# Ranks stage of a Perceiver-Mamba kernel: where key rows lie, which engine folds weights, and how the counting loops are written

## The chip, the cores and the metric

One core of a Trainium2 chip runs the whole program in one launch. The metric is the device time of one execution in microseconds. Five engines run at once, each through its own list of instructions, and are tied together by semaphores: TensorE (PE, with its weight loads PEld), VectorE (DVE), ScalarE (ACT), GpSimd (POOL) and SyncE (SP), which here only issues transfers. ScalarE issues a few transfers too.

## The reference

A layer of three blocks works on 16 x 32 tokens of 512 channels: a point-cloud cross attention, a Mamba-2 block and a small gated feed-forward. Only the start of the first block matters here. Its coordinates are three rows of the context; they are quantised to 10 bits, turned into four space-filling-curve keys per point (two Morton, two Hilbert), and each key list is sorted:

```
def _sorted_indices(coords_bn3):
    q = _quantize(coords_bn3)
    qt = q[..., jnp.array([1, 0, 2])]
    keys = [_morton_key(q), _morton_key(qt), _hilbert_key(q), _hilbert_key(qt)]
    return [jnp.argsort(kk, axis=1) for kk in keys]
...
x = x + _L0_xattn_ref(ctx_4096, _layernorm(x, axis=-1), ...)
```

The sorted order is used to gather windows of 10 neighbours out of the layer-normed `x` (the latents). `W_lin1`, `W_lin2` with `W_conv1`, `W_conv2` follow; since they are linear one after the other they can be multiplied together beforehand.

## The kernel before

The function `keys_and_ranks` is the first stage; barriers and cleared semaphores separate it from the next, `gather_windows`. It never sorts. It finds the rank of every key by comparing it with all the others of its list: 16 batches of 512 keys for each of 4 curves.

**Keys.** VectorE quantises, spreads bits and forms the Morton keys (`pieces(0)`), then the Hilbert keys (bit loops, then `pieces(1)`). A key is cut into three fp16 pieces plus an index row, four rows in all (`p16`). SyncE stores them in DRAM (`store_keys`, L200) and they come back transposed by `load_keys` (L188): into `mv_key` and `st_key`, four small transfers of two partitions for each curve, so eight for the Morton pair (four issued by SyncE, four by ScalarE) and eight for the Hilbert pair (all on SyncE). Curve m has its eight rows at partitions 32m to 32m+7: key rows in one tile face constant rows in the other, which ScalarE filled before (L318).

**Differences.** TensorE multiplies eight rows of `st_key` by eight of `mv_key` (L268): the product at (i, j) is key j minus key i. By symmetry only the upper triangle is made, 512, 384, 256 and 128 columns for tiles 0 to 3, of both curves of a pair. These lie in three PSUM banks (`TURNS`: tile 0, tile 1, tiles 2 and 3).

**Counting.** For the first nine Morton batches (`SOLO`) ScalarE takes the sign of both curves with a row sum (L332). After that a batch is shared: ScalarE takes curve one (L340 Morton, L348 Hilbert), VectorE compares curve two with zero and counts (L496, L504). I call the 7 Morton and 16 Hilbert batches of this kind the shared batches, 23 in all. TensorE then adds up columns of the signs for the other triangle (`column_sums`, L282, one column each). The two engines' counting loops are hardware loops (`Fori`) whose waits and addresses are computed from a loop register. TensorE's part is written out. TensorE waits until a bank is counted before it writes it again, and takes column sums two steps behind the differences.

**Work on the side.** Layer norm of the latents: VectorE makes statistics, ScalarE the root, VectorE then writes `latn` (L470) after the Hilbert keys. Folded weights: TensorE multiplies them at the start (L238 to L242), and after `latn` VectorE scales them by their largest entry and splits them (L478 to L487), 18 instructions for two layers. TensorE transposes the result two steps into the Hilbert half (L303), and VectorE copies that out after its last count (L509, L542, L543). VectorE's order is a list written by hand: Hilbert keys, `latn`, weights, shared Morton batches, Hilbert batches, weight copies, and last the ranks from counts and column sums (L516 to L528). GpSimd has nothing to do in the stage.

## Time and profile before

| what | us |
|---|---|
| median of three runs (lowest, highest) | 2252.63 (2251.91, 2253.1) |
| the profiled execution | 2251.6 |
| its span | 2249.8 |
| VectorE begins to write `latn` | 64.37 |
| first count by VectorE | 71.07 |
| last count by VectorE ends | 118.8 |
| first VectorE instruction of the next stage | 126.14 |

The span is what the profiler saw between the first and the last instruction, and the execution's time is 1.8 us more. All times below are from the span's start. In the timeline a piece's start and length are given, and in brackets how long the engine was idle before it and who released it. A matmul's end is modelled, so that starts are the better measure on TensorE. The stage at issue is the first 126 us; in it TensorE's granted clock is at its full level throughout. The chain that the page gives as having ended last covers only the last stage, and so this stage has to be read from timelines and waits.

### The profile page before, as it was taken

Reading aid. Unit: us, or ns where it says so; the run is one execution under the profiler, and the core shown is the slowest. Engines: PE = TensorE matmul, PEld = TensorE weight load, DVE = VectorE, ACT = ScalarE, POOL = GpSimd, SP = SyncE. Lnnn points to the kernel's source line nnn. Section 1 sums busy time; section 2 is a strip of 40 time slices with the busy share of each in tenths; the row PEclk is TensorE's granted clock in tenths of the full one; section 3 lists DMA queues with packets and bytes.
Section 4 is the critical chain, followed back from the end, with each engine's and each line's share of the span. In section 5 each row is a group of like instructions: output and inputs, shape, how many; then the busy total and the mean of one; then the engine's idle time right before and its main releaser. Section 6 shows DMA issues by size and latency. Waiting matters only on the chain. (4 is left out here: it accounts for less than half of the span.)

```text
span 2249.8 us, 100270 instructions
## 1 busy us (share of the span) xinstructions
PE 1857.1 (83%) x37656; PEld 1296.1 (58%) x37656; DVE 1865.7 (83%) x3775; ACT 1620.7 (72%) x3324; POOL 1007.2 (45%) x995
## 2 busy tenths in 40 slices
PE   3866648888886665699999997687999999999957
PEld 1333347777775433599999996333544454454422
DVE  8879969999997798688888887865888888888874
ACT  5889948888886998699999996465455455555432
POOL 0000048999995000578888884002433444344412
PEclk9996679999998666899999998899999999999988
DMA  1127666555563477645555551203222222222210
GB/s 36 30 65 169 163 146 126 119 125 122 120 125 72 94 171 164 133 101 107 107 107 107 107 107 38 95 10 96 85 80 84 75 84 81 82 84 75 65 55 19
DMA packets 434892, 215.50 MB, mean 96 GB/s; under 512 B 301195, under 2 KB 404267, under 8 KB 434680
## 3 DMA queue, kind: packets, MB, share of 16 engines
q1 hardware_dynamic: 430272, 210.76, 39.8%
q10 hardware_dynamic: 4536, 3.66, 0.6%
q8 instruction: 48, 0.79, 0.2%
q14 instruction: 36, 0.29, 0.0%
HBM read 161.35 MB, written 52.86 MB: 95 GB/s over the span
## 5 line engine op out<-in xcount | busy, mean ns | idle before, releaser
L973 PE MATMUL pQ<-QM,QX 128*128 128x64 f16 (+1 forms) x5760 | 532.4, 217 | 1.6 <-issue 1.6
L971 PE MATMUL pQ<-neigh_lo,QX 128*128 128x32 f16 (+1 forms) x5760 | 520.9, 189 | 2.8 <-issue 2.8
L971 PEld LDWEIGHTS pQ<-neigh_lo,QX 128*128 128x128 f16 x5760 | 496.0, 103 | 5.2 <-issue 2.5
L973 PEld LDWEIGHTS pQ<-QM,QX 128*128 128x128 f16 x5760 | 487.8, 104 | 2.5 <-issue 2.3
L1069 POOL TENSOR_TENSOR Dm<-Sc,mx 128x450 f32<-128x450 f32 x384 | 365.9, 953 | 80.6 <-DVE mx L1029 80.6
L1076 POOL TENSOR_TENSOR Ap<-E,R 128x450 f32<-128x450 f32 x384 | 365.8, 953 | 68.0 <-DVE R L1042 57.8
L1106 ACT ACTIVATE Vs<-pQ 128x480 f32<-128x480 f32 (+1 forms) x384 | 295.7, 770 | 5.7 <-PE pH L999 4.1
L1038 DVE STREAM_TRANSPOSE AT<-Ap 128x480 f32<-128x480 f32 x384 | 259.2, 675 | 33.3 <-PE pH L999 10.9
L2067 POOL TENSOR_TENSOR MT<-cb,decay 128x512 f32 (+1 forms) x128 | 163.9, 1302 | 244.2 <-PEq L1835 147.4
L1119 ACT ACTIVATE E<-Dm 128x450 f32<-128x450 f32 x384 | 224.3, 584 | 60.5 <-POOL Dm L1069 60.4
L1029 DVE TENSOR_REDUCE mx<-Sc 128x15 f32<-128x450 f32 x384 | 223.8, 583 | 16.5 <-ACT Sc L1100 16.5
L1033 DVE TENSOR_REDUCE Z<-E 128x15 f32<-128x450 f32 x384 | 233.5, 608 | 0.0
L1100 ACT ACTIVATE Sc<-pQ 128x450 f32<-128x450 f32 x384 | 209.2, 545 | 14.7 <-PE pQ L973 14.6
L999 PE MATMUL pH<-AT,Vs 128*32 128x30 f32 x17280 | 177.2, 197 | 47.5 <-DVE AT L1038 41.9
L999 PEld LDWEIGHTS pH<-AT,Vs 128*32 128x32 f32 x17280 | 172.5, 110 | 67.8 <-DVE AT L1038 42.0
L707 DVE TENSOR_TENSOR QT<-ext,cen 128x1710 f16<-128x1710 f32 x96 | 180.6, 1936 | 28.5 <-ACT ext L795 23.9
L966 PE MATMUL pQ<-maskR,maskL 128*128 128x160 f16 (+1 forms) x960 | 143.1, 247 | 67.5 <-DMA QX<-scratch_q 40.5
L2082 POOL TENSOR_TENSOR sqsum<-sqsum,sq 128x512 f32<-128x512 f32 x56 | 85.0, 1518 | 245.4 <-ACT sq L1928 245.4
L1860 PE MATMUL pO<-Wo,yw 128*128 128x512 f16 x768 | 176.3, 379 | 13.9 <-DVE Wo L2025 13.9
L1842 PE MATMUL pG<-h,W 128*128 128x512 f16 x768 | 178.2, 382 | 9.3 <-DVE W L2049 8.4
L2035 DVE SCALAR_TENSOR_TENSOR cv_m<-pX,taps_m,cv_m 128x496 f32<-128x496 f32 (+2 forms) x192 | 137.6, 717 | 51.7 <-ACT cv_m L1937 33.5
L1942 ACT ACTIVATE hid<-cv_m 128x512 f32<-128x512 f32 x64 | 40.3, 630 | 189.5 <-DVE cv_m L2035 189.5
(382 smaller groups left out, 3743.3 us busy)
## 6 DMA issues: line engine op xcount, KB each, us to landing
QM<-scratch_q SPq DMA_DIRECT2D x192, 240.0 KB, 2.7
QX<-scratch_q SPq DMA_DIRECT2D x768, 60.0 KB, 2.4
scratch_q<-QT SPq DMA_DIRECT2D x120, 360.0 KB, 4.8
Wg<-in_in_proj SPq DMA_DIRECT2D x64, 256.0 KB, 2.7
Wh<-in_in_proj SPq DMA_DIRECT2D x64, 256.0 KB, 2.8
Wo<-in_out_proj SPq DMA_DIRECT2D x64, 256.0 KB, 2.7
W_s<-in_in_proj SPq DMA_DIRECT2D x16, 256.0 KB, 2.7
CT<-scratch_c SPq DMA_DIRECT2D x192, 11.2 KB, 2.2
```

The costliest lines, as they stand in the source:

```text
L707: v.tensor_tensor(flat[:, 0:W3, n * K:(n + 1) * K, :], rows(ext, k, LEAD * K + HALF - 1 + n, (PTS * RES, W3), (1, K), (PTS, RES)), rows(ce ...
L971: nc.tensor.matmul(pQ[:, p, u // PB, o + 32:o + BW], qx[u], W["neigh_lo"][:, 0:O], start=False, stop=True, skip_group_check=True)
L973: last = nc.tensor.matmul(pQ[:, p, u // PB, o:o + BW], qx[u], qm[u], start=False, stop=True, skip_group_check=True)
L999: last = nc.tensor.matmul(pH[at0:at0 + 32, p, 32 * u:32 * u + PTS * K], Vs[:, first + slot, u * O + 32 * half:u * O + 32 * half + 32], AT[ ...
L1029: v.tensor_reduce(mx[:, p, :], valid(Sc[:, p, :]), X, ALU.max).then_inc(max_ready, 1)
L1033: v.tensor_reduce(Z[:, p, :], valid(E[:, p, :]), X, ALU.add).then_inc(summed, 1)
L1038: v.transpose(AT[:, k5 % NA, :], A[:, k5 % ND, :]).then_inc(turned, 1)
L1069: nc.gpsimd.tensor_tensor(valid(Dm[:, p, :]), valid(Sc[:, p, :]), mx[:, p, :].unsqueeze(2).to_broadcast([128, SUBS, PTS * K]), ALU.subtrac ...
L1076: nc.gpsimd.tensor_tensor(valid(A[:, p, :]), valid(E[:, p, :]), R[:, p, :].unsqueeze(2).to_broadcast([128, SUBS, PTS * K]), ALU.mult).then ...
L1100: nc.scalar.activation(like(Sc[:, (k - 1) % ND, :], 32, PTS * K), blocks(p, 0, PTS * K), ACT.Copy)\
L1106: nc.scalar.activation(like(Vs[:, kv % RV, :], O, O), blocks(p, 32, O), ACT.Copy).then_inc(vs_ready, 1)
L1119: nc.scalar.activation(valid(E[:, p, :]), valid(Dm[:, p, :]), ACT.Exp, scale=32.0 ** -0.5).then_inc(exped, 1)
```

## The change

Four things change, all in `keys_and_ranks` and its constants.

1. `load_keys` moves all eight rows of a curve pair in one transfer. They now lie eight partitions apart (`mv_key` at 0, 8, ..., 56, `st_key` at 4, 12, ..., 60, plus 64 for the Hilbert pair). A pair needs two transfers instead of eight. The constants `units` are laid out accordingly, with zeros elsewhere, and each difference now contracts 32 rows instead of 8.
2. The counting loops of ScalarE and VectorE are written out, with constants in their waits. `SOLO` goes from 9 to 10, so 22 batches are shared.
3. GpSimd writes `latn`, scales and splits the folded weights, copies the transposed ones out, and makes the Morton ranks. Since it works from SBUF, ScalarE copies the folded product (`raws`) and the transposed weights (`sides`) out of PSUM. VectorE takes the two maxima and reciprocals at once, ahead of the Morton keys.
4. TensorE transposes the weights before the first difference. Column sums of the Hilbert pair go to the bank `pw`; VectorE copies the Morton sums out (`early`) after its second Hilbert batch, and at the end finishes the Hilbert ranks alone.

```diff
-        SOLO = 9
+        SOLO = 10
...
-        def load_keys(eng, m):
-
-            for h in range(2):
-                for tile, at in ((mv_key, 32 * m + 4 * h), (st_key, 32 * m + 4 * h + 2)):
-                    eng.dma_start(tile[at:at + 2, :, 0:N],
-                                  scratch["pk"][m, 2 * h:2 * h + 2, :].rearrange("r (b n) -> r b n", b=B))\
-                        .then_inc(keys_in[m // 2], 16)
+        def load_keys(eng, curve, tile, at):
+
+            eng.dma_start(tile[64 * curve + at:64 * curve + 64:8, :, 0:N],
+                          scratch["pk"][2 * curve:2 * curve + 2].rearrange("m r (b n) -> (m r) b n", b=B))\
+                .then_inc(keys_in[curve], 16)
...
-                                                st_key[32 * m:32 * m + 8, b, t * 128:t * 128 + 128],
-                                                mv_key[32 * m:32 * m + 8, b, t * 128:N], start=True, stop=True)
+                                                st_key[32 * m:32 * m + 32, b, t * 128:t * 128 + 128],
+                                                mv_key[32 * m:32 * m + 32, b, t * 128:N], start=True, stop=True)
...
+                if tile is mv_key:
+                    act.wait_ge(folded, 1)
+                    nc.scalar.activation(raws[:, :], pw[:, 0:2 * (C + 129)], ACT.Copy).then_inc(raw_ready, 1)
...
+            act.wait_ge(turned, 1)
+            nc.scalar.activation(sides[:, :], pw[:, 0:6 * C], ACT.Copy).then_inc(sides_ready, 1)
...
-            load_keys(act, 1)
-            with act.Fori(0, SOLO) as b:
+            load_keys(act, 0, st_key, 4)
+            for b in range(SOLO):
...
+            dve.wait_ge(raw_ready, 1)
+            for l, W in enumerate(weights):
+                raw = raws[:, l * (C + 129):(l + 1) * (C + 129)]
+                link(v.tensor_reduce(W["amax"][:, :], raw[:, 0:C + 128], X, ALU.max, apply_absolute_value=True), l == 1)
...
-            with dve.Fori(0, B) as b:
+            for b in range(B):
...
+                if b == 1:
+                    v.tensor_copy(early[:, :, :], part[:, :, :]).then_inc(morton_sums, 1)
...
+            pool.wait_ge(rstd_ready, 1)
+            for t in range(4):
+                g.tensor_scalar(latn[:, t, :], lat[:, t, :], mv[:, t, 0:1], rstd[:, t:t + 1],
+                                ALU.subtract, ALU.mult).then_inc(latn_ready, 1)
+            pool.wait_ge(morton_sums, 1)
```

VectorE's list between the last key pieces (`p`) and its first counts, before:

```order
L387 TENSOR_SCALAR p<-pf 128x2x64 x3
L533 RECIPROCAL rstd<-sd 128x4
...
L470 TENSOR_SCALAR latn<-lat,mv,rstd 128x512 x4
L478 COPY bias<-pw 128x1
L479 TENSOR_REDUCE amax<-pw 128x1
...
L487 TENSOR_SCALAR eff<-pw,inv 128x128
L490 UNCONDITIONAL_BRANCH
```

and the same place now, with the two lines of six instructions that stand further up, before the Morton keys:

```order
L433 BN_STATS bst<-lat 128x6 x3
L437 TENSOR_REDUCE amax<-raws 128x1 x2
L439 TENSOR_SCALAR amax<-amax 128x1 x2
L441 RECIPROCAL inv<-amax 128x1 x2
L447 COPY A<-qin 128x2x64 x6
...
L401 TENSOR_SCALAR p<-pf 128x2x64 x3
L573 RECIPROCAL rstd<-sd 128x4
...
L577 TENSOR_TENSOR rstd<-rstd,rtmp 128x4
L497 TENSOR_SCALAR less,rank<-diff 128x512
```

Between the keys and the first count 22 instructions are gone, and six stand ahead of the Morton keys.

VectorE's loop of one shared Hilbert batch, before (`ISA` and `REGISTER_ALU` rows compute addresses and wait values):

```order
L498 UNCONDITIONAL_BRANCH
L498 ISA
L502 ISA
L504 ISA
L504 TENSOR_SCALAR less,rank<-diff 128x512
...
L504 TENSOR_SCALAR less,rank<-diff 128x128
L498 REGISTER_ALU
L498 COMPARE_AND_BRANCH
```

and now:

```order
L505 TENSOR_SCALAR less,rank<-diff 128x512
L505 TENSOR_SCALAR less,rank<-diff 128x384
L505 TENSOR_SCALAR less,rank<-diff 128x256
L505 TENSOR_SCALAR less,rank<-diff 128x128
L508 COPY early<-sums 128x192
```

The branch and its arithmetic are gone, and `early` stands once, behind the second Hilbert batch.

## Rows read from the trace of the kernel before

**Rows 1.** Busy by stretch: length, PE, PEld, DVE, ACT, POOL, clock, DMA share, GB/s

```profile
35.54:65.08 29.54, 19.36 (x180) 7.75 (x176) 29.30 (x204) 29.54 (x144) 0.00 (x0) 1.00 0.03 5
...
71.07:85.42 14.35, 13.29 (x134) 5.95 (x134) 12.34 (x57) 11.08 (x49) 0.00 (x0) 1.00 0.31 97
...
85.42:88.18 2.76, 2.76 (x26) 1.46 (x24) 1.82 (x9) 1.92 (x9) 0.00 (x0) 1.00 0.03 6
```

**Rows 2.** Timeline of VectorE: start us, us, engine, line, operation, tiles, count, idle before

```profile
64.37 2.30 DVE L470 TENSOR_SCALAR latn<-lat,mv,rstd 128x512 f32<-128x512 f32 x4
...
66.58 0.15 DVE L478 COPY bias<-pw 128x1 f32<-128x1 f32 x1
...
71.07 0.69 DVE L496 TENSOR_SCALAR_CACHE_REDUCE less<-diff 128x512 f16<-128x512 f32 x1
```

**Rows 3.** Waits, 60 to 90 us: who waited for whom, total, times, longest

```profile
PE sums L282 <- DVE less L496: 5.4, 1, 5.4
ACT sign L340 <- PE sums L282: 6.7, 6, 5.6
```

**Rows 4.** Timeline of VectorE and TensorE between 10 and 15 us

```profile
13.94 0.42 PE L242 MATMUL pw<-blin,convT 64*128 64x1 f32 x2
14.22 0.90 DVE L425 COPY A<-qin 128x128 int32<-128x128 int32 x6 [1.75 <-DMA qin<-ci]
```

**Rows 5.** First key load: issues, one window during it, first difference

```profile
23.01 0.77 SPq L188 DMA_DIRECT2D mv_key<-scratch_pk  x1
26.00 0.70 ACTq L188 DMA_DIRECT2D st_key<-scratch_pk  x1
...
29.00:30.00 1.00, 0.00 (x0) 0.00 (x0) 1.00 (x9) 0.00 (x0) 0.00 (x0) 1.00 0.14 31
...
34.71 0.61 PE L268 MATMUL diff<-mv_key,st_key 8*128 8x512 f16 x2 [20.35 <-DMA st_key<-scratch_pk]
```

**Rows 6.** Timeline of one shared batch: TensorE and VectorE, Hilbert half

```profile
104.30 0.08 DVE L504 DVE_READ_ACCUMULATOR less<-diff  x1
...
104.47 0.50 PE L268 MATMUL diff<-mv_key,st_key 8*128 8x384 f16 x2
...
104.67 0.69 DVE L504 TENSOR_SCALAR_CACHE_REDUCE less<-diff 128x512 f16<-128x512 f32 x1 [0.28 <-PE sums L282]
```

**Rows 7.** Timeline of TensorE: starts of the difference groups of one shared batch

```profile
111.97 0.60 PE L268 MATMUL diff<-mv_key,st_key 8*128 8x512 f16 x2
...
112.71 0.50 PE L268 MATMUL diff<-mv_key,st_key 8*128 8x384 f16 x2
...
113.29 0.50 PE L268 MATMUL diff<-mv_key,st_key 8*128 8x256 f16 x4
...
113.98 0.60 PE L268 MATMUL diff<-mv_key,st_key 8*128 8x512 f16 x2
```

**Rows 8.** Timeline of VectorE at the end of the stage

```profile
118.74 0.19 DVE L509 CAST center<-pw 128x32 f16<-128x32 f32 x1
...
120.57 0.11 DVE L516 MEMSET below<- 128x64 f32 x1 [0.41 <-DVE neigh_lo L543]
...
123.00 1.26 DVE L528 SCALAR_TENSOR_TENSOR rank<-rank,below 128x7 f32<-128x7 f32 x6
...
126.14 0.06 DVE L677 MEMSET unit_g<- 128x1 f32 x1 [1.88 <-PEq L53]
```

**Rows 9.** Timeline of the last stage: GpSimd and VectorE both reading SBUF

```profile
2196.93 1.26 POOL L2313 TENSOR_TENSOR uf_f<-uf_f,u_f 115x512 f32<-115x512 f32 x1 [37.40 <-DVE u_f L2280]
...
2197.55 1.20 DVE L2285 TENSOR_TENSOR u_f<-u_f 115x512 f16<-115x512 f32 x1 [0.70 <-ACT u_f L2224]
```

**Rows 10.** Instructions of one line, L2285: duration ns min/median/max

```profile
L2285 DVE TENSOR_TENSOR u_f<-uf_f,u_f x3: 692/693/693, 2195.6 to 2220.1; 115x512 f16<-115x512 f32 x3
```

**Rows 11.** Groups of GpSimd instructions by form: busy us, mean ns, idle before

```profile
L1069 POOL TENSOR_TENSOR Dm<-Sc,mx 128x450 f32<-128x450 f32 x384 | 365.9, 953 | 80.6 <-DVE mx L1029 80.6
...
L665 POOL MEMSET cen<- 128x4 f32 x2 | 0.2, 104 | 146.8 <-POOLq L53 146.8
```

More of the change, by code:

```diff
@@ L153, in keys_and_ranks @@
         sums = ctx.enter_context(nc.psum_tensor("sums", [128, 512], F32))
+        part, late = (bank[:, 0:2 * B * len(PAIRS)].rearrange("p (x k) -> p x k", k=len(PAIRS)) for bank in (sums, pw))
+        turns = tally[:, :, :, :].rearrange("p m b t -> p (m b) t")
         lat_in = sem("lat_in")
@@ L216, in _ @@
             sp.wait_ge(filled, 2)
-            load_keys(sp, 0)
+            load_keys(sp, 0, mv_key, 0)
             sp.wait_ge(keys_ready, 6)
@@ L280, in column_sums @@
                     for t2 in range(t + 1, NT):
-                        at = ((2 * curve + e) * B + b) * len(PAIRS) + PAIRS.index((t, t2))
-                        last = nc.tensor.matmul(sums[:, at:at + 1], rows[:, t2 * 128:t2 * 128 + 128], ones[:, :],
+                        at = (e * B + b) * len(PAIRS) + PAIRS.index((t, t2))
+                        last = nc.tensor.matmul((sums, pw)[curve][:, at:at + 1], rows[:, t2 * 128:t2 * 128 + 128], ones[:, :],
                                                 start=True, stop=True)
                 last.then_inc(summed, 1)
-            pe.wait_ge(keys_in[0], 16 * 8)
+            pe.wait_ge(scaled, 2)
+            for l, W in enumerate(weights):
+                O = W["O"]
+                for side in range(2):
+                    last = nc.tensor.transpose(pw[:, 2 * C * l + side * O:2 * C * l + (side + 1) * O],
+                                               eff[0:O, l, side, :, :].rearrange("p c m -> p (c m)"), ident[0:O, 0:O])
+            last.then_inc(turned, 1)
+            pe.wait_ge(keys_in[0], 16 * 2)
+            pe.wait_ge(sides_ready, 1)
             pe.wait_ge(ones_ready, 1)
@@ L297, in _ @@
                     column_sums(s - 2)
-                if s == STEPS // 2 + 2:
-                    pe.wait_ge(scaled, 2)
-                    for l, W in enumerate(weights):
-                        O = W["O"]
-                        for side in range(2):
-                            last = nc.tensor.transpose(pw[:, 2 * C * l + side * O:2 * C * l + (side + 1) * O],
-                                                       eff[0:O, l, side, :, :].rearrange("p c m -> p (c m)"),
-                                                       ident[0:O, 0:O])
-                    last.then_inc(turned, 1)
         @block.scalar
@@ L430, in _ @@
             v.tensor_scalar(mv[:, :, 1], mv[:, :, 1], EPS, None, ALU.add).then_inc(var_ready, 1)
-            link(v.memset(eff[:, :, 0, :, :].rearrange("p l c m -> p l (c m)"), 0.0), False)
             def ax(e, k):
@@ L496, in _ @@
                         v.tensor_scalar(less[:, t, t * 128:N], bank[:, 1, c0:c0 + N - t * 128], 0.0, 0.0, ALU.is_lt,
-                                        ALU.add, accum_out=rank[:, bass.ds(b + B, 1), t]).then_inc(counted, 1)
-            with dve.Fori(0, B) as b:
+                                        ALU.add, accum_out=rank[:, B + b, t:t + 1]).then_inc(counted, 1)
+            for b in range(B):
                 for i, tiles in enumerate(TURNS):
@@ L521, in _ @@
-            turns = tally[:, :, :, :].rearrange("p m b t -> p (m b) t")
-            for r0, r1 in ((0, B + SOLO), (2 * B, 3 * B)):
-                link(v.tensor_tensor(turns[:, r0:r1, :], turns[:, r0:r1, :], below[:, r0:r1, :], ALU.subtract))
-                link(v.tensor_scalar(rank[:, r0:r1, :], turns[:, r0:r1, :], -0.5, (N - 1) / 2.0, ALU.mult, ALU.add))
-            for r0, r1 in ((B + SOLO, 2 * B), (3 * B, 4 * B)):
-                for t in range(1, NT):
-                    last = rank[:, r0:r1, t]
-                    link(v.scalar_tensor_tensor(last, last, 128.0 * t, below[:, r0:r1, t], ALU.add, ALU.subtract))
+            h = slice(2 * B, 4 * B)
@@ new lines, in _ @@
+            link(v.memset(below[:, h, 0], 0.0), False)
+            link(v.tensor_copy(below[:, h, 1:3], late[:, :, 0:2]), False)
+            link(v.tensor_reduce(below[:, h, 3], late[:, :, 2:6:2], X, ALU.add))
+            link(v.tensor_tensor(below[:, h, 2], below[:, h, 2], late[:, :, 3], ALU.add), False)
+            link(v.tensor_tensor(below[:, h, 3], below[:, h, 3], late[:, :, 5], ALU.add))
+            one, two = slice(2 * B, 3 * B), slice(3 * B, 4 * B)
+            link(v.tensor_tensor(turns[:, one, :], turns[:, one, :], below[:, one, :], ALU.subtract), False)
```

120 lines of the change are left out of this document (74 added, 46 removed).

## The prediction, made before the changed kernel had run

> **What bounds the kernel now.** The stage at issue is followed by a barrier and everything behind it is unchanged, so what counts is when VectorE finishes the ranks. I read the table by stretch first. While ScalarE counts nine Morton batches alone it is busy for all of 29.54 us, 3.28 a batch, and VectorE, making Hilbert keys, is busy for 29.30 [rows 1]. Two chains thus run side by side, and the wait list says which ends last: TensorE waits once for 5.4 us for VectorE's first count, and ScalarE, which has counted one batch ahead, once for 5.6 us behind it [rows 3]. VectorE is late. Its timeline says why: `latn` begins at 64.37, the weights at 66.58, the first count at 71.07 [rows 2]. From there to the end of the last count at 118.74 + 0.08 = 118.82 (the weight copies start as its accumulator read does) lie 47.75 us for 23 shared batches. One pair of steps in it is odd: the first Hilbert batch takes 2.76 us [rows 1], since TensorE's four transposes stand behind it. Without that excess of 0.7 a batch is 2.046. The tail from 118.82 to the last rank at 123.00 + 1.26 = 124.26 is 5.44 us, and the next stage starts 1.88 later [rows 8].
>
> So the path is: VectorE's keys, its 6.7 us of side work, 23 shared batches, the tail. The first key load is not on it.
>
> **VectorE's start (gain 2.9 us).** The first count stands at 71.07. Without `latn` and weights it could come 0.1 after 64.37 [rows 2], 6.6 earlier. Against that stands what is put in before the Morton keys. TensorE's fold ends at 13.94 + 0.42 = 14.36 [rows 4]. ScalarE then copies 322 columns out of PSUM; a solo batch's eight passes over 2560 columns take 3.28, so 320 columns cost 0.41 [rows 1], and with two handovers of 0.1 VectorE gets them at 14.97. Six instructions follow. The old fold took 71.07 - 66.58 = 4.49 for 18 [rows 2], 0.25 each, two of these six without a wait: 1.4. The Morton keys start at 16.4 and not at 14.22 [rows 4], 2.15 later, less about 0.15, my estimate for one small memset of `eff` that goes to GpSimd. That is 2.0.
>
> The unknown is GpSimd. In the key part it now runs 18 instructions, 16 on up to 64 columns and two on 128, while VectorE's key steps mostly take two operands from SBUF. The nearest rows on GpSimd are 0.104 us for four columns and 0.953 for 450 with two inputs [rows 11], so 0.1 to 0.25 for a small one and 0.2 to 0.42 for 128 columns: 2.0 to 4.8 us busy in all. Does that stop VectorE? In the last stage a subtraction with both inputs in SBUF takes 1.20 us when GpSimd's addition has begun 0.62 earlier, and 0.69 otherwise [rows 9, 10]; it ends 0.56 after GpSimd does, so it stood until then. The price lies between nothing, if GpSimd runs in gaps, and the whole 4.8. I take 1.7, half of the middle, since VectorE also has single-input steps, and GpSimd's handovers leave it alone. First count: 64.37 + 0.1 + 2.0 + 1.7 = 68.2, and 71.07 - 68.2 = 2.9. Bounds 66.5 and 71.3.
>
> The Trainium skill (SBUF — State Buffer, "SBUF: two separate sides") says that GpSimd and a VectorE instruction with two SBUF inputs lock a shared port for the whole instruction. The trace agrees. It speaks against this part of the change; by it alone the price would be near the full busy time.
>
> **Is ScalarE ready by then?** With ten solo batches it has to be asked. The Morton store and loads come 2.0 to 2.2 later from the insertion and about 1 from GpSimd's share: first load issued at 23.01 + 3.2 = 26.2 instead of 23.01 [rows 5]. From issue to first difference are 11.7 us now; one window inside has a DMA share of 0.14 at 31 GB/s [rows 5]. 0.14 of 16 engines are 2.2, for transfers of two rows each. 256 KB at that rate are 8.5 us, which leaves 3.2 for issue and latency. Transfers of eight rows could use four times the engines: 2.1, total 5.3. TensorE starts at 31.5, ScalarE 0.83 later (35.54 after 34.71, [rows 1, 5]), and ends ten batches at 31.5 + 0.83 + 32.8 = 65.1. That is 3 us before VectorE, so the faster transfer costs and gains nothing by itself; it pays for the tenth solo batch. Behind it lie GpSimd's folded weights: TensorE now waits for `scaled`, and its differences are queued behind that. Twelve instructions at up to 0.35 with their waits from 16.4 are done at 20.6, transposes 0.7 [rows 1], ScalarE's copy 0.4: 21.7, under the 26.2 of the load. ScalarE's own load is queued behind the wait for `turned`; 4 us of room.
>
> The skill (DMA: Bandwidth & Descriptors, "Why a DMA increments its semaphore by 16 and not by 1") says that the engine count is the largest number up to 16 that divides both patterns' slowest dimensions: two before, eight now. The share of 0.14 agrees with two of 16; it would give the same 2.1.
>
> The Hilbert store comes 3.7 later, near 67.2, its loads on SyncE are in by some 67.2 + 2.2 + 0.6 + 5.3 = 75.3, and they are wanted from about 79. `latn` on GpSimd runs beside VectorE's counts, which read PSUM; at up to 1.1 each (953 ns for 450 columns, [rows 11]) the four end by 73. SyncE waits for the fourth, and behind it only the store of `latn` is queued, read after the barrier. Both hidden, with 4 and 30 us of cover.
>
> **The shared batches (gain 3.75).** One batch less is 2.05, the transposes another 0.7. What is left is the written-out loop. VectorE stands 0.28 between its last accumulator read (104.30 + 0.08) and the next batch's first count at 104.67 [rows 6]. If only that went, a batch would take 2.046 - 0.28, about 1.8. But TensorE's groups start 0.74, 0.58 and 0.69 apart, 2.01 in sum [rows 7], without a reported wait between them, so I take TensorE to be the next limit, at 2.00. 22 x 2.00 = 44.0 against 47.75 is 3.75. Bounds: 22 x 1.8 = 39.6 (TensorE's groups shrink) and 22 x 2.046 + 0.36 = 45.4 (nothing from the loops, and the copy `early` fully paid: 192 columns at the 0.69 of 512 [rows 6] are 0.26, with 0.1 for its start 0.36). I count `early` at nothing, since VectorE has that 0.28 of slack in every batch; without slack it costs the 0.36. Wider row groups (32 for 8) stream the same columns, which I put at nothing too.
>
> **The tail (gain 3.1).** Now 5.44. The weight copies go, 120.57 - 118.74 with their wait [rows 8]; the wait for the last column sums stays, the 0.41 of idle in front of the first rank instruction [rows 8]. From 120.57 to 124.26 are 15 instructions in 3.69, 0.25 each; 10 are left on half the columns, five of them without a wait, at 0.19: 1.9. New tail 2.3 to 2.4. The Morton ranks on GpSimd, some 13 instructions from about 77 + 4, are long done. Barrier and clears: seven more semaphores on five engines, 0.1 lost.
>
> **Sum.** 2.9 + 3.75 + 3.1 - 0.1 = 9.65. The profiled execution took 2251.6, so 2241.95; the median of the runs lies 1.0 above it: **2242.9**, 0.43% faster.
>
> **Rivals.**
> - *The key load stays slow.* If eight rows move no faster than two, the first difference comes at 26.2 + 11.7 = 37.9, ScalarE ends solo at 71.5, and VectorE can start only some 0.8 before that, at 70.7 rather than 68.2. 2245.4. For it: nothing but the lack of such a transfer in the trace. Against: the share of 0.14.
> - *GpSimd stops VectorE for all its busy time*, 3.1 us more: 2246.0. For it: [rows 9]. Against: VectorE's single-input steps. It is the port rule of the skill taken in full.
> - *TensorE is not the next limit.* A batch falls to 1.8: 4.4 us more gained, 2238.5. For it: TensorE's sums start just after VectorE's accumulator read ends. Against: its 2.01 with no wait reported.
> - *TensorE gets slower*, the side of a loss. 32-row differences, or a granted clock that falls to 1.2 GHz, would cost up to the 2560 columns once more, 1.07 us a batch at 2.4 GHz; 22 batches are 23.5: 2266.4. It decides from 0.44 us a batch, where the gain of 9.65 is gone. For it: no row has such a 32-row fp16 difference. Against: the clock column is 1.00 in every stretch [rows 1], and the columns are the same.
> - *The loops' code must be fetched and stalls* would be a change that doesn't do what it says; TensorE's list of this stage is already written out and shows no such stall. Within the bounds of 2.046.
>
> **How the numbers follow.** Forecast 66%, slow load 10%, full port price 13%, lower limit 8%, slower TensorE 3%. About 0.2% (4.5 us) is what a measurement of this kernel can tell from no change. Faster by over that means below 2248.1: the first four cases less the corner where slow load and full price meet, 92%; within 5%; slower 3%. The range takes in the third rival, 2238.5, and above the two middle ones with a little of their sum: 2248.0.
>
> **What would show it.** Right: first difference near 31.5; first VectorE count near 68, before it a wait of ScalarE and not of VectorE; batches of 2.00 with TensorE never idle; 2.4 us from the last count to the last rank; the next stage near 116. Wrong: VectorE's key steps stretched one by one beside GpSimd; a DMA share of 0.14 after the issue; ScalarE counting solo when VectorE is ready; batches at 2.05 or 1.8; GpSimd at Morton ranks when VectorE ends.

## The result, and the profile of the changed kernel

| | before | changed |
|---|---|---|
| median, us (lowest to highest, runs) | 2253.11 (2251.91 to 2258.57, 6) | 2243.77 (2241.66 to 2245.11, 6) |
| ratio, 95% interval | | 0.995 (0.9937 to 0.9963) |
| profiled execution, and its span | 2251.6, 2249.8 | 2243.7, 2241.9 |
| VectorE's first count | 71.07 | 66.90 |
| VectorE's last count ends | 118.82 | 110.64 |
| next stage starts | 126.14 | 114.25 |

The changed kernel is faster by 0.5%, some 11 us by the ratio (8 to 14 by its interval) and 9.3 by the two medians. The stage itself became 11.9 us shorter, where the prediction had summed 9.65.

VectorE's timeline of the changed kernel, in the three places that [rows 2, 4, 8] show of before: the maxima ahead of the Morton keys, the first count, the end of the stage.

```profile
15.13 0.55 DVE L437 TENSOR_REDUCE amax<-raws 128x1 f32<-128x160 f32 x2 [2.68 <-ACT raws L331]
...
16.10 0.88 DVE L447 COPY A<-qin 128x128 int32<-128x128 int32 x6
...
66.90 0.69 DVE L497 TENSOR_SCALAR_CACHE_REDUCE less<-diff 128x512 f16<-128x512 f32 x1 [0.25 <-DVE rstd L577]
...
110.56 0.08 DVE L505 DVE_READ_ACCUMULATOR less<-diff 128x1 f32 x1
111.06 0.19 DVE L515 COPY below<-pw 128x64 f32<-128x64 f32 x1 [0.42 <-ACT sign L362]
...
112.33 0.20 DVE L524 TENSOR_SCALAR rank<-tally 128x64 f32<-128x64 f32 x1
114.25 0.06 DVE L717 MEMSET unit_g<- 128x1 f32 x1 [1.73 <-PEq L53]
```

Six instructions stand ahead of the Morton keys, 16.10 instead of 14.22. No `latn` and no weights stand ahead of the first count. Behind the last accumulator read there are only ranks: 110.64 to 112.53, 1.9 us instead of 5.44.

Stretches of the changed kernel, with the columns of [rows 1]: ScalarE's ten solo batches, one us of the key load, 30 us of shared batches.

```profile
29.93:62.70 32.77, 21.71 (x200) 8.78 (x196) 32.77 (x236) 32.77 (x161) 0.00 (x0) 1.00 0.01 2
27.00:28.00 1.00, 0.00 (x0) 0.00 (x0) 1.00 (x8) 0.00 (x0) 0.00 (x0) 1.00 0.44 147
80.00:110.00 30.00, 30.00 (x303) 13.30 (x301) 27.71 (x121) 29.07 (x121) 3.40 (x13) 1.00 0.01 2
```

The same 30 us in the kernel before:

```profile
80.00:110.00 30.00, 29.55 (x294) 13.39 (x292) 25.28 (x115) 27.08 (x115) 0.00 (x0) 1.00 0.01 2
```

TensorE is now busy for 30.00 of 30 us. VectorE (27.71 for 25.28) and ScalarE (29.07 for 27.08) have come up with it, in part because more batches lie in the same time (14.7 of 2.046 before, 15.1 of 1.988 now). From 66.90 to 110.64 are 43.74 us for 22 batches, 1.988 each.

The load, in the timelines of SyncE's queue, TensorE and ScalarE (compare [rows 5]):

```profile
25.26 0.70 SPq L199 DMA_DIRECT2D mv_key<-scratch_pk  x1
...
29.30 1.25 PE L279 MATMUL diff<-mv_key,st_key 32*128 32x512 f16 x8 [6.86 <-DMA st_key<-scratch_pk]
...
29.93 0.60 ACT L346 ACTIVATE sign<-diff 128x512 f16<-128x512 f32 x1 [5.27 <-PE diff L279]
```

From issue to first difference it takes 4.0 us where it took 11.7. ScalarE has done ten batches at 62.70, 4.2 us before VectorE's first count: VectorE is still the late one.

GpSimd, in its timeline of the changed kernel: two steps of the second layer's weights, the last of the copies out of `sides`, the four `latn`, the first and the last of the Morton ranks.

```profile
19.34 0.54 POOL L537 TENSOR_SCALAR both<-raws,inv 128x32 f32<-128x32 f32 x1
...
20.92 0.64 POOL L542 TENSOR_SCALAR eff<-raws,inv 128x128 f32<-128x128 f32 x1
...
26.33 0.30 POOL L583 TENSOR_TENSOR neigh_lo<-sides,neigh_hi 128x64 f16<-128x64 f32 x1
66.89 8.25 POOL L551 TENSOR_SCALAR latn<-lat,mv,rstd 128x512 f32<-128x512 f32 x4 [40.25 <-DVEq L490]
82.88 0.16 POOL L557 MEMSET below<- 128x32 f32 x1 [7.75 <-DVE early L508]
...
87.06 0.21 POOL L567 TENSOR_TENSOR rank<-rank,below 128x6 f32<-128x6 f32 x1
```

Its 18 instructions in the key part are busy for 5.9 us (4.39 for twelve from 16.36, 1.54 for six from 24.73). All of GpSimd's work ends at 87.3, 23 us before VectorE's last count.

### The profile page after: what moved, and what is told of

The parts are those of the page before. It is cut to its first block and busy times, and to the rows that moved or that the text cites. A ratio compares the mean times of both kernels' runs of the same rounds, so it can differ in the third digit from the quotient of the medians.

```text
span 2241.9 us, 99712 instructions
## 1 busy us (share of the span) xinstructions
PE 1860.9 (83%) x37656; PEld 1298.0 (58%) x37656; DVE 1858.9 (83%) x3740; ACT 1623.9 (72%) x3334; POOL 1025.4 (46%) x1031
```

## The experiments

Each ran beside the kernel before on the same chip; "stage end" is the first VectorE instruction of the next stage, and "behind it" is the profile's span less that. The kernel before had a median of 2252.79 beside the first four, 2252.75 beside the second four and 2252.01 beside the last four.

| kernel | median | ratio to before (95%) | first difference | first count | stage end | behind it |
|---|---|---|---|---|---|---|
| before | 2253.11 | | 34.71 | 71.07 | 126.14 | 2123.7 |
| changed | 2243.77 | 0.995 (0.9937 to 0.9963) | 29.30 | 66.90 | 114.25 | 2127.7 |
| again | 2241.71 | 0.9943 (0.9922 to 0.9963) | 29.34 | 66.71 | 113.78 | 2126.1 |
| solo11 | 2239.56 | 0.9928 (0.9907 to 0.9949) | 29.52 | 66.74 | 111.92 | 2127.0 |
| fori | 2244.32 | 0.9954 (0.9938 to 0.997) | 29.14 | 66.81 | 115.38 | 2126.7 |
| two_rows | 2245.37 | 0.9962 (0.9945 to 0.998) | 33.23 | 66.79 | 114.19 | 2127.9 |
| before_again | 2254.05 | 1.0002 (0.9988 to 1.0015) | 34.72 | 71.22 | 126.23 | 2131.6 |
| load_alone | 2250.53 | 0.9991 (0.9979 to 1.0002) | 27.52 | 71.18 | 126.08 | 2125.9 |
| latn_dve | 2242.92 | 0.9959 (0.9941 to 0.9978) | 29.57 | 68.27 | 115.22 | 2126.4 |
| pool_more | 2249.68 | 0.9987 (0.9974 to 1.0) | 29.82 | 73.20 | 120.23 | 2127.5 |
| delay | 2258.13 | 1.0027 (1.0016 to 1.0038) | 29.61 | 66.80 | 129.22 | 2128.4 |
| pool_single | 2244.35 | 0.9969 (0.9958 to 0.9979) | 29.54 | 71.55 | 118.49 | 2124.3 |
| solo10_alone | 2251.08 | 0.9997 (0.9983 to 1.0012) | 34.62 | 71.04 | 123.84 | 2125.6 |
| solo12 | 2242.02 | 0.9958 (0.9945 to 0.9971) | 29.59 | 69.24 | 113.22 | 2125.6 |

The stage end of one kernel repeats within 0.5 us (114.25 and 113.78, 126.14 and 126.23), while medians are uncertain by some 3. So the stage end is what tells most of these apart.

**again**: the changed kernel once more, the baseline of its group.

> The changed kernel once more, unaltered. In its first profile the next stage began at 114.25 us, 11.9 us earlier than before, but the span fell by 7.9 only: 4.0 us are given back later, and the profile shows them where TensorE's granted clock was at its lower level for groups that ran at the higher one before (a group of 12 matmuls pO at 2140.8 took 4.3 us for 2.76, another at 2151.0 the same, and the first pG group 5.3 for 4.1). Theory: the stage itself gives 11.9 every time, start of the next stage at 114.2 to 114.3 again; what follows it (2127.7 us of the span in that profile, 2123.7 in the one of before) differs from execution to execution by some microseconds with the places at which the clock falls. Rival: the give-back belongs to the change and is fixed, 2127.7 again within 0.5 us. Time: 2242 to 2245 by both.

It repeats the result. The two profiles differ by 0.5 at the stage end.

### Which engine is late, and by how much: solo batches

**solo11**

```diff
-        SOLO = 10
+        SOLO = 11
```

> One constant: SOLO is 11, ScalarE counts eleven Morton batches alone and 21 are shared. In the changed kernel ScalarE is through with its ten at 62.7 us and VectorE's first count comes at 66.9, so 4.2 us are free and one batch costs ScalarE 3.28. Theory (VectorE's keys still end last there): first count stays near 66.9, or up to 0.3 later, one shared batch of 1.99 less, next stage at 112.3 to 112.6 for 114.25, time 2 us less, 2241 to 2243. Rival (ScalarE's solo part already sets the start): first count moves 3 us later, the next stage comes at 115 or later.

Stage end 111.92, 2.3 and 1.9 before the two profiles of ten. VectorE's timeline shows that there was just room:

```profile
66.32 0.16 DVE L577 TENSOR_TENSOR rstd<-rstd,rtmp 128x4 f32<-128x4 f32 x1
66.74 0.69 DVE L497 TENSOR_SCALAR_CACHE_REDUCE less<-diff 128x512 f16<-128x512 f32 x1 [0.25 <-PE diff L279]
```

The first count is as early as with ten, but the bank of its batch is released by TensorE in the same moment as VectorE has done its last `rstd`. By its stage end this is the fastest kernel of the study; its median is the lowest too, but its interval overlaps with those of again and solo12.

**solo12**: the same with 12.

> The changed kernel with twelve solo batches instead of ten (eleven gave a next stage at 111.92, 2.3 earlier than ten). ScalarE ends them at 29.93 + 12 x 3.28 = 69.3, VectorE is ready at 66.9. Theory: VectorE now waits some 2.4 for the bank of its first batch and has one batch less of 1.98, so the next stage comes at 112.0 to 112.6, no better than eleven; first count at 69.2. Rival (TensorE's lead lets VectorE start at once): 109.9.

```profile
66.40 0.16 DVE L577 TENSOR_TENSOR rstd<-rstd,rtmp 128x4 f32<-128x4 f32 x1
69.24 0.69 DVE L497 TENSOR_SCALAR_CACHE_REDUCE less<-diff 128x512 f16<-128x512 f32 x1 [2.68 <-PE diff L279]
```

In VectorE's timeline the wait for TensorE has grown to 2.68, and one batch less does not pay for it: stage end 113.22, 1.3 after eleven. The first count came as forecast; the 20 batches behind it (to 109.61) took 2.02 each, a little more than forecast, which is the 0.6 by which the end was missed.

**solo10_alone**: the kernel before with SOLO = 10 and nothing else.

> The kernel before with ten solo batches instead of nine and nothing else: the slow load and the loops stay. ScalarE then ends solo at 65.1 + 3.3 = 68.4, still before VectorE's first count at 71.1. Theory (one shared batch less, 2.05): next stage at 124.1 instead of 126.2, so the tenth solo batch did not need the faster load. Rival (ScalarE has to be two or more batches ahead, so the tenth makes VectorE wait): next stage at 125.2 or later.

Stage end 123.84, 2.3 earlier. So the tenth solo batch needed neither the faster load nor the written-out loops. The prediction said that the faster load "pays for the tenth solo batch". It does not: even with the slow load there was room for ten. The median of this kernel is 0.9 below that of before, with an interval that holds both 0 and 2.3; the trace shows what the median cannot.

### The key load

**load_alone**: the kernel before with the new layout and the two transfers a pair, nothing else.

```diff
-            for h in range(2):
-                for tile, at in ((mv_key, 32 * m + 4 * h), (st_key, 32 * m + 4 * h + 2)):
-                    eng.dma_start(tile[at:at + 2, :, 0:N],
...
+            eng.dma_start(tile[64 * curve + at:64 * curve + 64:8, :, 0:N],
...
-                                                st_key[32 * m:32 * m + 8, b, t * 128:t * 128 + 128],
+                                                st_key[32 * m:32 * m + 32, b, t * 128:t * 128 + 128],
```

> The kernel before with one part of the change: key rows eight partitions apart, two transfers for a curve pair, 32-row contractions. Loops, SOLO = 9, latn and weights stay as before. Theory: the load takes 4.0 us from first issue to first difference instead of 11.7, so the first difference stands near 27.0 instead of 34.71 and ScalarE's solo batches end near 58; but VectorE's first count stays at 71.1 +- 0.3, a batch at 2.05 (wider row groups cost nothing), the next stage at 126.1 +- 0.3, and the time is that of before. Rival 1 (the load is on the path): the next stage comes 3 us or more earlier. Rival 2 (32-row contractions cost TensorE time): the batches grow above 2.08 and the next stage comes later than 126.8.

In the timelines of TensorE and VectorE:

```profile
27.52 1.25 PE L266 MATMUL diff<-mv_key,st_key 32*128 32x512 f16 x8 [13.26 <-DMA st_key<-scratch_pk]
...
71.18 0.69 DVE L494 TENSOR_SCALAR_CACHE_REDUCE less<-diff 128x512 f16<-128x512 f32 x1
```

The first difference comes 7.2 us earlier, and the first count and the stage end (126.08) do not move. The load is not on the path. The 23 batches take 47.71 us against 47.75: contracting 32 rows costs what 8 did.

**two_rows**: the changed kernel with its layout, but two rows a transfer, eight transfers a pair.

```diff
-            eng.dma_start(tile[64 * curve + at:64 * curve + 64:8, :, 0:N],
-                          scratch["pk"][2 * curve:2 * curve + 2].rearrange("m r (b n) -> (m r) b n", b=B))\
-                .then_inc(keys_in[curve], 16)
+            for m in range(2):
+                for h in range(2):
+                    p0 = 64 * curve + 32 * m + 16 * h + at
+                    eng.dma_start(tile[p0:p0 + 9:8, :, 0:N],
+                                  scratch["pk"][2 * curve + m, 2 * h:2 * h + 2, :].rearrange("r (b n) -> r b n", b=B))\
+                        .then_inc(keys_in[curve], 16)
```

> The changed kernel with the key rows at their new places but brought by eight transfers of two rows a curve pair, as many bytes and as many transfers as before. Theory (what counts is how many rows a transfer has, since it uses as many DMA engines): a DMA share near 0.13 while they run, from first issue to first difference 11 to 12 us for 4.0, first difference near 37, ScalarE's ten solo batches then end near 70.4, VectorE's first count 2 to 3.5 us later than 66.9, next stage at 116.5 to 117.8. Rival (the place of the rows, eight partitions apart, is what makes them fast): first difference before 32 and next stage at 114.3.

Both expectations missed the first difference: it is at 33.23, 8.1 us after the first issue at 25.16. The theory's DMA share (0.13) and the rival's stage end (114.3) came. Two stretches during the load:

```profile
28.00:29.00 1.00, 0.00 (x0) 0.00 (x0) 1.00 (x9) 0.00 (x0) 0.00 (x0) 1.00 0.13 47
29.00:30.00 1.00, 0.00 (x0) 0.00 (x0) 1.00 (x9) 0.00 (x0) 0.00 (x0) 1.00 0.13 45
```

The kernel before, in its slowest and its fastest full us of the same load:

```profile
27.00:28.00 1.00, 0.00 (x0) 0.00 (x0) 1.00 (x9) 0.00 (x0) 0.00 (x0) 1.00 0.14 23
...
30.00:31.00 1.00, 0.00 (x0) 0.00 (x0) 1.00 (x9) 0.00 (x0) 0.00 (x0) 1.00 0.13 43
```

A share of 0.13 is two engines of sixteen, as it was before (0.13 to 0.14), but they move 45 to 48 GB/s from 28 to 32 us where they moved 23 to 43, on average 31, from 26 to 33 us. The one us in [rows 5] was thus a middling one. So there are two effects: two rows eight partitions apart load faster than two adjacent ones on as many engines, and eight rows in a transfer bring a share of 0.44 and 147 GB/s. The Trainium skill (DMA: Bandwidth & Descriptors, "Why a DMA increments its semaphore by 16 and not by 1") gives the number of engines from the slowest dimension, eight and two here. The shares agree with it: 0.13 is 2.1 engines of sixteen, and 0.44 is seven busy on average in that us. What makes the two engines faster was not taken apart further. The stage end is that of the changed kernel (114.19), since ScalarE still has time: it has done its ten batches at about 66.6 (33.87 + 32.77, as long as in the changed kernel), and the first count is at 66.79.

### The loops

**fori**: the changed kernel with hardware loops on ScalarE and VectorE again, for example

```diff
-            for b in range(SOLO, B):
+            with dve.Fori(SOLO, B) as b:
...
-                                        ALU.add, accum_out=rank[:, B + b, t:t + 1]).then_inc(counted, 1)
+                                        ALU.add, accum_out=rank[:, bass.ds(b + B, 1), t]).then_inc(counted, 1)
```

> The changed kernel with the counting loops of ScalarE and VectorE as hardware loops again (with VectorE's Hilbert loop in two pieces, 2 and 14 batches, around the copy of the Morton sums), all else as changed. Theory of the prediction (TensorE is the next limit, the loop costs only what stands over it): a shared batch goes from 1.99 to 2.05 us, the next stage starts 1.0 to 1.6 us later, near 115.5. Rival (VectorE's loop head is on the path in full, 0.28 us a batch): 6 us later, near 120.4. Second rival (loops cost nothing): 114.3.

From 66.81 to 111.63 are 44.82 us, 2.037 a batch, and the stage ends 1.1 to 1.6 later. Its stretch of shared batches and one turn of VectorE:

```profile
80.00:110.00 30.00, 29.72 (x294) 13.00 (x294) 26.02 (x120) 27.98 (x119) 3.42 (x13) 1.00 0.00 1
...
91.06 0.08 DVE L514 DVE_READ_ACCUMULATOR less<-diff  x1
91.42 0.69 DVE L514 TENSOR_SCALAR_CACHE_REDUCE less<-diff 128x512 f16<-128x512 f32 x1 [0.28 <-PE pw L293]
```

The same turn of the changed kernel:

```profile
90.50 0.08 DVE L505 DVE_READ_ACCUMULATOR less<-diff 128x1 f32 x1
90.73 0.69 DVE L505 TENSOR_SCALAR_CACHE_REDUCE less<-diff 128x512 f16<-128x512 f32 x1 [0.15 <-PE diff L279]
```

With the loop VectorE stands for 0.28 a turn. Written out it still stands for 0.15, but now for TensorE's difference, which is not there yet. Taking the loops away therefore gives 0.05 a batch and not 0.28: TensorE is the next limit.

Where the 0.05 arises can be read on TensorE. In the changed kernel its three groups of differences start 0.74, 0.58 and 0.69 apart in every turn from 80 to 110 us. With the loops the third distance is about 0.77 in every second turn and 0.70 in the others, because TensorE's column sums wait for ScalarE's sign. Such a turn, in the timeline of fori:

```profile
91.73 0.50 PE L279 MATMUL diff<-mv_key,st_key 32*128 32x256 f16 x4
...
92.24 0.16 PEld L293 LDWEIGHTS pw<-ones_r,sign 128*128 128x128 f16 x3 [0.38 <-ACT sign L362]
...
92.50 0.61 PE L279 MATMUL diff<-mv_key,st_key 32*128 32x512 f16 x2
```

The same wait in the wait lists from 80 to 110 us, first of the changed kernel, then of fori:

```profile
PEld pw L293 <- ACT sign L362: 6.5, 15, 0.4
```

```profile
PEld pw L293 <- ACT sign L362: 11.8, 30, 0.4
```

The kernel before shows the same beat, 0.70 and 0.80 by turns. So what the loops cost seems to reach TensorE through ScalarE's loop rather than VectorE's; since fori puts back both at once, this is read from the timeline and was not tested.

### GpSimd beside VectorE

**latn_dve**: `latn` back on VectorE.

```diff
-            dve.sem_inc(rstd_ready, 1)
+            for t in range(4):
+                v.tensor_scalar(latn[:, t, :], lat[:, t, :], mv[:, t, 0:1], rstd[:, t:t + 1],
+                                ALU.subtract, ALU.mult).then_inc(latn_ready, 1)
```

> The changed kernel with the four latn instructions moved back from GpSimd to VectorE, behind its Hilbert keys. Theory: GpSimd's four (8.25 us in the profile) were hidden and cost VectorE nothing; on VectorE they are 2.3 us on the path: first count at 69.2 instead of 66.9, next stage at 116.5 instead of 114.25, time 2.3 above the changed kernel. Rival (GpSimd's latn slows VectorE's counts, or TensorE has no room to take them up): moving it back costs under 1 us, next stage at 115.2 or earlier.

The first count is at 68.27, 1.4 to 1.6 later, and the stage end at 115.22, 1.0 to 1.4 later. The direction is that of the theory, but the size lies at the rival's bound (115.2, under 1). The rival's first reason does not hold: VectorE's first counts take 0.69 beside GpSimd's `latn` as they do without it. VectorE's timeline says why the step is smaller than the theory's:

```profile
66.44 1.92 DVE L491 TENSOR_SCALAR latn<-lat,mv,rstd 128x512 f32<-128x512 f32 x4
68.27 0.68 DVE L499 TENSOR_SCALAR_CACHE_REDUCE less<-diff 128x512 f16<-128x512 f32 x1
```

The four take 1.83 and not 2.3, and the 0.25 that VectorE waits behind `rstd` in the changed kernel is gone. Between first count and stage end another 0.1 to 0.4 is made up; the 22 batches take 43.35 for 43.47 to 43.74. What GpSimd does in 8.25 us is thus worth 1.0 to 1.4 on VectorE.

**pool_more**: 24 additions on GpSimd during VectorE's Hilbert keys.

```diff
+            for k in range(24):
+                link(g.tensor_tensor(spare[:, :], sides[:, 0:128], raws[:, 0:128], ALU.add))
             pool.wait_ge(rstd_ready, 1)
```

> The changed kernel with 24 additions of 128 columns with both inputs in SBUF put on GpSimd behind its weight work, so while VectorE makes Hilbert keys; each some 0.3 us, about 8 us of GpSimd's busy time. In the changed kernel 5.9 us of GpSimd's work beside the keys cost VectorE 0.6. Theory (GpSimd costs VectorE a tenth of its busy time): first count 0.5 to 1.2 later than 66.9, time at most 1.2 above the changed kernel. Rival (while GpSimd works on two SBUF inputs VectorE stands): first count 6 to 8 later, near 74, time 2250. Second rival (no price at all): first count within 0.2 of 66.9.

VectorE's first count is at 73.20, 6.3 later, and the median is 2249.68. These are the first rival's numbers (6 to 8 later, 2250), but not its mechanism: it had VectorE stand through some 8 us of GpSimd's work, and the additions fill 12.83. GpSimd and VectorE in their timelines:

```profile
26.73 12.83 POOL L551 TENSOR_TENSOR spare<-sides,raws 128x128 f32<-128x128 f32 x24
...
28.79 0.67 DVE L461 TENSOR_SCALAR pos<-A 128x192 int32<-128x192 int32 x2
...
29.91 0.61 DVE L466 TENSOR_TENSOR u<-A 128x64 int32<-128x64 int32 x2
30.44 0.61 DVE L467 SCALAR_TENSOR_TENSOR u<-u,pos 128x64 int32<-128x64 int32 x2
```

The same three lines in the changed kernel:

```profile
27.72 0.41 DVE L460 TENSOR_SCALAR pos<-A 128x192 int32<-128x192 int32 x2
...
29.68 0.34 DVE L465 TENSOR_TENSOR u<-A 128x64 int32<-128x64 int32 x2
29.95 0.34 DVE L466 SCALAR_TENSOR_TENSOR u<-u,pos 128x64 int32<-128x64 int32 x2
```

A pair of key steps takes 0.53 from start to start where it takes 0.27, and the additions follow each other every 12.83 / 24 = 0.53. In each turn VectorE gets two steps through instead of four: it loses 6.3 / 24 = 0.26 an addition, half of its time. It does not stand for the whole of GpSimd's busy time, and it is far from free. The single-input step (`pos`) is held up as well, 0.67 for 0.41, so such steps were not the shelter for which the prediction took them.

**pool_single**: 24 copies of 256 columns in that place, one input each.

```diff
+            for k in range(24):
+                link(g.tensor_copy(spare[:, :], raws[:, 0:256]))
             pool.wait_ge(rstd_ready, 1)
```

> The changed kernel with 24 copies of 256 columns on GpSimd beside VectorE's Hilbert keys, one SBUF input each; some 10 us of GpSimd's work. The 24 additions with two inputs of the run before cost VectorE 6.3 us in 12.8. Theory (only GpSimd's two-input instructions hold VectorE's two-input ones up): first count at most 1.2 later than 66.9, VectorE's pairs of key steps at 0.34 to 0.37. Rival (any GpSimd work on SBUF costs half of its time): first count 4 to 6 later, pairs at 0.5 to 0.6.

```profile
26.57 11.36 POOL L551 COPY spare<-raws 128x256 f32<-128x256 f32 x24
...
29.40 0.55 DVE L466 TENSOR_TENSOR u<-A 128x64 int32<-128x64 int32 x2
29.87 0.55 DVE L467 SCALAR_TENSOR_TENSOR u<-u,pos 128x64 int32<-128x64 int32 x2
```

My theory fell and the rival held (4 to 6 later, pairs at 0.5 to 0.6): copies slow VectorE too, and the pairs of key steps take 0.55. The first count is at 71.55, 4.65 later, 0.19 for each copy of 11.36 / 24 = 0.47. The number of inputs on GpSimd does not decide. A common reading, which these runs don't prove, is that the engines take turns: in each turn VectorE runs its two steps, 0.27, and then stands for 0.19 or 0.26, and the turn is the sum of both, 0.47 or 0.53. GpSimd would hold it up only for the part of an instruction in which its columns pass, not for the fixed part, most of a small instruction. By that, a column costs 0.19 / 256 = 0.76 ns copied and 0.26 / 128 = 2.1 ns added; the 18 instructions of the changed kernel cover some 640 columns with one input and 160 with two, 0.5 + 0.3 = 0.8 us, near the 0.6 measured (below). [Rows 9] give a third width that fits: the addition of 512 columns began 0.62 before VectorE's subtraction, which then took 1.20 for 0.69, so that it was held until 0.62 + 0.51 = 1.13 into the addition's 1.26; 512 columns at 2.1 ns are 1.08. It stays an argued reading; no run doubled one width and left the rest alone.

The Trainium skill (SBUF — State Buffer, "SBUF: two separate sides") says that a GpSimd instruction that reads SBUF and a VectorE instruction with two SBUF inputs lock each other out for the whole instruction. The turns agree with the lock, for copies as well; its length does not agree, since VectorE lost 0.19 and 0.26 of turns of 0.47 and 0.53, in which one copy lasts 0.41 and one addition 0.455.

### Where the rest of the time is

**before_again**: the kernel before, profiled a second time. The reason: in the first pair of profiles the changed kernel is 11.9 ahead at the stage end but only 7.9 at the end of the span, and the granted clock is at different levels in the later stages. A stretch of `pO` groups in the changed kernel, and the stretch of the kernel before that holds the same groups:

```profile
2149.90:2154.90 5.00, 3.88 (x12) 1.62 (x13) 1.06 (x1) 0.42 (x1) 0.51 (x1) 0.72 0.00 0
```

```profile
2159.00:2164.00 5.00, 3.55 (x20) 2.14 (x20) 1.32 (x3) 0.45 (x1) 0.53 (x1) 1.00 0.01 3
```

> The kernel before, once more, with a profile of its own. What is asked: the time from the first VectorE instruction of the next stage to the end of the span. It was 2123.7 us in the one profile of before, and 2126.1 to 2127.9 in five profiles of kernels of the new kind, whose code behind the stage is the same. Theory (the profile of before was a quick one, the rest varies from execution to execution with the granted clock): this second profile has a rest of 2125 to 2128. Rival (the earlier start really costs something later): it stays within 0.7 of 2123.7. The stage itself: next stage at 126.1 +- 0.3.

Behind the stage it takes 2131.6, not 2123.7: the code is the same, and two executions differ by 7.9. The theory that it varies holds, its range was too narrow. The timelines show where the 7.9 lie. VectorE's `la_f` (L2297), its last step before the four last results, starts at 2230.11 in before and at 2229.85 in before_again, so up to there the two agree within 0.4. What is left takes 19.7 and 27.9. In that last stretch TensorE's granted clock differs. A window of it in before, and the wait of VectorE for the second of the four results:

```profile
2240.00:2249.80 9.80, 5.46 (x20) 1.77 (x17) 1.38 (x2) 0.00 (x0) 0.00 (x0) 0.96 0.22 80
...
2239.29 0.69 DVE L2300 SCALAR_TENSOR_TENSOR res_f<-pg_f,acc 128x512 f32<-128x512 f32 x1 [2.41 <-PE pg_f L2379]
```

and in before_again:

```profile
2240.00:2249.80 9.80, 9.80 (x19) 2.70 (x18) 1.38 (x2) 0.00 (x0) 0.00 (x0) 0.50 0.07 27
...
2242.61 0.69 DVE L2300 SCALAR_TENSOR_TENSOR res_f<-pg_f,acc 128x512 f32<-128x512 f32 x1 [5.26 <-PE pg_f L2379]
```

Results follow each other every 3.10 at the upper level, and at the lower one twice after 5.95; the last comes after 4.94, when the clock has risen again. All thirteen other profiles take 19.2 to 19.7 for this stretch.

The four profiles with the old code behind the ranks (before, before_again, load_alone, solo10_alone) have 2126.7 on average behind the stage, the ten others 2126.8. But this equality rests on that one slow stretch. From stage end to `la_f` the four take 2105.0 on average (2103.6 to 2106.3) and the ten 2107.4 (2105.2 to 2108.9). So of the 4 us that seemed to be given back in one pair of profiles some 2 are scatter, and some 2 may be real.

**delay**: the changed kernel with 13 fills on VectorE between the last count and the ranks.

```diff
+            for k in range(13):
+                link(v.memset(spare[:, :], 0.0))
             h = slice(2 * B, 4 * B)
```

> The changed kernel with 13 fills of 1024 columns on VectorE between the last count and the ranks, 0.91 us each by the 858 ns of a fill of 960 columns: the stage ends some 12 us later, near 126, where it ended before the change. What is asked: of the 12 us that the stage gains, 9 to 10 reach the total; is that because what follows starts earlier, or because the changed kernel's later stages are slower in themselves? Theory (the start decides: the granted clock of later stages falls otherwise): the total returns to that of the kernel before, within 1 us, although the stage ends at the same time. Rival (the later part is slower whenever it starts, or the medians of the earlier runs merely scatter): the total is that of the changed kernel plus the full 12, so 2 to 3 us above the kernel before.

I had left out the 0.28 between two chained fills, so that each took 1.19, and the stage ended 15.0 later and not 12, at 129.22. The time is 6.1 above before by the medians (3.6 to 8.6 by the interval), for a stage end 3.1 later; above the changed kernel and its repetition it is 14.4 and 16.4. So the total follows the stage end. The theory would have wanted about 3.1 above before, just outside the interval; the rival 5 to 6. By the medians, time less stage end is 2126.6 on average for the kernels of old code and 2128.6 for those of new code, each kernel from 2.7 us below to 2.6 above its group's average. Two us are therefore probably lost somewhere behind the stage: the medians say 2.0 and the profiles up to `la_f` 2.3. The earlier start is not the reason, since delay, whose stage ends later than that of before, has the largest value of all up to `la_f`, 2108.9. The reason stays open.

## Why the prediction was right, point by point

The median of 2243.77 is 0.9 above the 2242.9 forecast. That it is so close is luck. The stage gained 2.25 more than the sum, and some 2 us seem to be lost behind it, where the prediction took everything as unchanged; besides, one pair of medians can't tell 2 us. The mechanism and each term are judged by the stage alone:

- **What bounds.** Right. VectorE's late first count, its 23 batches and its tail were the path: load_alone moves the load by 7.2 and the end by nothing, solo10_alone takes a batch off and the end moves by 2.3.
- **VectorE's start: 4.2 instead of 2.9.** The insertion was sized well: 16.10 instead of the 16.4 forecast. The mis-sized step is GpSimd's price. The last `rstd` is done at 66.90 - 0.25 = 66.65 instead of 64.37, 2.3 later; 1.88 of it is the insertion, and 0.2 came back from the memset (from the last `mv` step to the first step on `A` behind it are 22.42 - 21.80 = 0.62 before and 24.45 - 24.04 = 0.41 now), so GpSimd cost 0.6 and I had put 1.7. The two halves of the estimate erred in opposite directions: GpSimd was busy for 5.9, above my bound of 4.8 (128 columns with a scalar for each partition took 0.64 to 0.69, I had allowed 0.42), and a busy us cost 0.1 where I had 1.7 for some 3.4. The lower bound of nothing was nearer than the middle. [Rows 9] showed a large addition against a large subtraction; pool_more shows that such sizes do cost half, the small instructions of the change little. The rival of the full busy time, 2246.0, was not met: VectorE lost 0.6 of the 5.9 that GpSimd was busy. That it goes by the columns is the reading argued under pool_single.
- **ScalarE ready.** Right, with more room: first difference at 29.30 (31.5 forecast; issue at 25.26 for 26.2, and 4.0 for 5.3), ten batches done at 62.70 (65.1). The 5.3 was 2.1 for the bytes and 3.2 for issue and latency; the bytes took about that (28, 147 and 87 GB/s in the three us from 26 to 29), so the 3.2 was too much. From this followed what solo11 confirms, an eleventh solo batch. The statement that the load pays for the tenth was wrong.
- **Hidden work.** Right in effect, wrong in size. `latn` took GpSimd 8.25 / 4 = 2.06 each, and I had at most 1.1 from an addition of 450 columns; it ended at 75.14 instead of 73. It was hidden, as latn_dve shows.
- **Shared batches: 4.0 instead of 3.75.** 1.988 each for 2.00. Of the 4.0, 2.0 to 2.3 are the batch less (solo10_alone, solo11), 1.1 the loops (44.82 - 43.74, fori; 1.35 against the repetition), and what is left, 0.6 to 0.9, answers to the transposes' 0.7. `early` was hidden, 32-row groups cost nothing.
- **Tail: 3.55 instead of 3.1**, and the barrier 1.72 instead of 1.88 where I had put 0.1 for more semaphores. Ten small instructions took 1.47 from the first to the end of the last, 0.15 each and not 0.19, with several of them written without a wait.

Together: 4.2 + 4.0 + 3.55 + 0.15 = 11.9, and 2.25 more than the sum. Of that, 1.1 is GpSimd's price (0.6 for 1.7); the rest of VectorE's start adds 0.2, the batches 0.25, the tail 0.45 and the barrier 0.25.

Of the rivals, the slow load was not met (DMA share 0.44), and would hardly have cost: with eight slow transfers of two rows ScalarE would still have been done by some 66.6 (62.70 + 33.23 - 29.30). Only at the 11.7 that the rival took from before would ScalarE have been late, at 25.26 + 11.7 + 0.63 + 32.77 = 70.4 for 66.90. TensorE was the next limit, busy for 30.00 of 30, with its groups at one and the same distance in every turn, and was not slowed: its clock stands at 1.00 in all of these stretches. The rival in which a batch falls to 1.8 left out ScalarE: it is busy for 29.07 of the 30, 1.93 a batch, so that (an estimate from this) the loops' end could not have brought a batch much below 1.9 even with a faster TensorE.

## What to carry over

Before work is moved to another engine, ask of each engine how late it is, in us, and give the slack away: one number (`SOLO`) was worth 2.3 us in the kernel before and 2.1 more in the changed one, more than the written-out loops or the move of `latn`. Moving small instructions to an idle GpSimd cost VectorE a tenth of their time, streams of 128 to 256 columns cost it 0.4 to 0.5 of theirs: move many small ones, or those that run beside VectorE's reads of PSUM, and measure the wide ones. Where one change moves the total by a fifth of a per cent, read the end of its stage in two profiles; it repeats within half a us where the total does not within three. And before two totals are compared, look at the granted clock stage by stage: one stretch of 20 us at the lower level made 8 us here.

## What the runs showed of the hardware

- Two engines' worth of DMA moved 45 to 48 GB/s into rows eight partitions apart and 23 to 43 (31 on average) into adjacent ones, at a share of 0.13 to 0.14 each; eight rows a transfer moved 147 GB/s.
- GpSimd beside VectorE's two-input key steps: additions of 128 columns come every 0.53 and cost VectorE 0.26 each, copies of 256 columns come every 0.47 and cost 0.19.
- GpSimd's instruction with two scalars for each partition takes 2.07 us for 512 columns, VectorE's 0.54; that is 4 ns a column, where its addition of 450 columns needs 2.1 [rows 11].
- The same kernel's later stages took 2123.7 us in one execution and 2131.6 in another. The difference lies in the last 20 to 28 us, where the granted clock was at 0.50 for most of the second, and results came after 5.95 for 3.10.
